# Ternary weights through GpSimd: the first of two operations moved, four G buffers, twelve places for up, the third weight summed in the first stage, attention rows loaded two tiles ahead

## The reference

```python
qkv = grouped_linear(x, w_qkv, None)           # 8 groups of 128 -> 384
out = softmax(q * D**-0.5 @ k.T) @ v           # 16 heads, D = 64, 2048 tokens
x = layernorm(x + grouped_linear(out, w_proj, b_proj))

def weight_quant(w):
    scale = 1.0 / clip(mean(abs(w)), 1e-5)     # one mean over all 4096 x 1024
    return clip(round(w * scale), -1, 1) / scale
def bitlinear(x, w): return act_quant(x) @ weight_quant(w).T
h = silu(bitlinear(x, w_gate)) * bitlinear(x, w_up)
y = layernorm(x + bitlinear(h, w_down))
```

## Time and profile before

| | us |
|---|---|
| three runs: median (lowest to highest) | 1289.52 (1288.72 to 1291.1) |
| the profiled execution, all cores | 1290.59 |
| its span on the slowest core (core 4) | 1289.0 |
| spans of the other cores | 1278.8 to 1287.9 |
| PE busy on core 4 | 1149.7 |
| DVE / ACT / POOL busy | 911.7 / 616.9 / 117.4 |

### The profile page before, as it was taken

How to read it: one execution, slowest core, us unless ns; L and a number is a source line. 1 busy time by engine, 2 the same in 40 slices (tenths; PEclk the granted TensorE clock), 3 DMA queues, 4 the chain that set the end, 5 groups by cost and what they waited for, 6 DMA issues and landing times.

```text
span 1289.0 us, 17877 instructions; the slowest of 8 cores (1278.8 to 1289.0 us)
## 1 busy us (share of the span) xinstructions
PE 1149.7 (89%) x6465; PEld 455.1 (35%) x6502; DVE 911.7 (71%) x1797; ACT 616.9 (48%) x679; POOL 117.4 (9%) x146
## 2 busy tenths in 40 slices
PE   3888998884898886599999999999999999999997
PEld 0333333321333222233333333333444444444443
DVE  4878889977899874474664547353789777977774
ACT  3798998884454487555555555554011111110110
POOL 1222112220001000010010001000000000000000
PEclk8999999997899898799999999999999999999999
DMA  8999934569799757242323223020523333233313
GB/s 237 307 326 316 325 102 158 176 195 318 239 250 226 208 138 241 90 92 65 92 70 78 86 39 117 5 70 1 145 89 81 89 82 99 72 89 66 82 34 82
DMA packets 129031, 179.74 MB, mean 139 GB/s; under 512 B 90033, under 2 KB 90801, under 8 KB 128946
## 3 DMA queue, kind: packets, MB, share of 16 engines
q1 hardware_dynamic: 120050, 149.52, 41.1%
q0 software_dynamic: 8896, 29.08, 7.4%
HBM read 127.41 MB, written 30.93 MB: 123 GB/s over the span
## 4 chain that ended last, share of the span: by engine, by line
PE 66%; DVE 13%; DMA 12%; ACT 5%; issue 4%; SPq 0%; POOL 0%; DVEq 0%; ACTq 0%; POOLq 0%
PE ps L802 32%; PE ps L897 16%; DMA stage<-wu 6%; PE ps L553 6%; PE ps L571 6%; PE ps L578 5%; ACT P L559 4%; DMA stage<-wd 3%; DVE asum L417 2%; DVE G L434 1%; ACT G L430 1%; DMA stage<-wg 1%; DMA stage<-xT 1%; DVE wgq L440 1%; DVE h L814 1%
## 5 line engine op out<-in xcount | busy, mean ns | idle before, releaser
L559 ACT ACTIVATE P<-ps 128x1024 bf16<-128x1024 f32 x512 | 492.5, 1021 | 236.6 <-PE ps L553 234.9
L808 ACT ACTIVATE T<-ps,tsc 128x512 f32<-128x512 f32 x128 | 88.0, 687 | 376.3 <-PE ps L802 330.5
L802 PE MATMUL ps<-wgq,xqT 128*128 128x512 fp8e4 x1024 | 249.2, 383 | 15.2 <-DVE hm L840 5.2
L802 PE MATMUL ps<-wuq,xqT 128*128 128x512 fp8e4 x1024 | 250.0, 384 | 8.7 <-DVE h L814 8.6
L897 PE MATMUL ps<-wdq,hqT 128*128 128x512 fp8e4 x1024 | 229.9, 380 | 1.3 <-DVE wdq L440 1.3
L571 PE MATMUL ps<-P,onesb 128*64 128x512 bf16 x1024 | 206.3, 399 | 14.2 <-DVE DT L594 14.2
L553 PE MATMUL ps<-Q,K 64*128 64x512 bf16 x1024 | 175.0, 389 | 44.1 <-ACT P L559 34.7
L578 PE MATMUL ps<-P,V 128*64 128x512 bf16 x1024 | 199.9, 386 | 0.9 <-DVE RC L598 0.5
L802 PEld LDWEIGHTS ps<-wuq,xqT 128*128 128x128 bf16 x1024 | 97.0, 99 | 142.0 <-issue 35.3
L802 PEld LDWEIGHTS ps<-wgq,xqT 128*128 128x128 bf16 x1024 | 95.8, 98 | 144.9 <-issue 39.9
L897 PEld LDWEIGHTS ps<-wdq,hqT 128*128 128x128 bf16 x1024 | 97.4, 98 | 129.8 <-issue 17.8
(11 more groups left out here) (95 smaller groups left out, 703.1 us busy)
## 6 DMA issues: line engine op xcount, KB each, us to landing
stage<-wu SPq DMA_DIRECT2D x64, 512.0 KB, 12.2
stage<-wd SPq DMA_DIRECT2D x58, 512.0 KB, 5.5
stage<-wg SPq DMA_DIRECT2D x42, 512.0 KB, 19.1
stage<-xT SPq DMA_DIRECT2D x16, 512.0 KB, 13.6
XB<-x SPq DMA_DIRECT2D x16, 512.0 KB, 5.3
xp_s<-XB SPq DMA_DIRECT2D x16, 512.0 KB, 2.6
Y<-xp_s SPq DMA_DIRECT2D x16, 512.0 KB, 4.3
y<-Y SPq DMA_DIRECT2D x16, 512.0 KB, 2.6
```

The costliest lines, as they stand in the source:

```text
L559: exp_tok[i] = act.do(lambda e: e.activation(P_sb[i % 4][:, :], bank(sb, 2), AF.Exp, bias=-C0, scale=0.125), pv_tok.get(i - 4), t)
L802: tp = pe.do(lambda e, ic=ic, w=w, bk=bk: e.matmul(bank(bk), xqT[b][:, ic, :], W_sb[w][:, 8 * q + ic, sl], start=(ic == 0), stop=(ic == 7) ...
L808: ta = act.do(lambda e: e.activation(T[:, :], bank(gb), AF.Tanh, bias=0.0, scale=tsc[:, t:t + 1]), tp, T_free[k], sc_tok[t])
```

## The change

1. Both first ternary operations (L434 on DVE, L430 on ACT) become one operation on POOL, for all three weights: 96 instructions.
2. The limit stays on DVE, but is emitted two pieces behind its first operation (`second`, `limit`), and there are four G buffers. Paid for with one RB buffer in place of two.
3. up's terns use 12 places (0 to 7 and 18 to 21) where they used 8.
4. The credit in the first stage is 0.62 for every step. A tern now costs 0.75 in all, where it cost 1.55.
5. Only places 22 and up are held back, so down's sums go through places 0 to 7 in the first stage.
6. The first stage ends after 252 steps; places 22 to 29 are released at step 230.
7. Two `AT` buffers; a tile's rows are loaded two tiles ahead.

```diff
-    AT = alloc("AT", [128, 8, 128], BF16)[0]
+    AT = [alloc(f"AT{i}", [128, 7, 128], BF16)[0] for i in range(2)]
-    G1 = [alloc(f"G1{i}", [128, 1024], I8)[0] for i in range(2)]
+    G1 = [alloc(f"G1{i}", [128, 1024], I8)[0] for i in range(4)]
-    RB = [alloc(f"RB{i}", [128, 512], F32)[0] for i in range(2)]
+    RB = alloc("RB", [128, 512], F32)[0]
...
-    order += [("tern", 1, k, k % 8, True) for k in range(16)]
+    ring = list(range(8)) + [18, 19, 20, 21]
+    order += [("tern", 1, k, ring[k % 12], True) for k in range(16)]
...
-    order += [("sum", 2, k, ring[n % 10], True) for n, k in enumerate(rest)]
+    order += [("sum", 2, k, n % 8, True) for n, k in enumerate(rest)]
...
-            if hold[0] and w == 2:
+            if hold[0] and s_ >= 22:
                 return
...
-            b = g1_n[0] % 2
+            b = g1_n[0] % 4
             g1_n[0] += 1
-            if w == 2:
-                t = act.do(lambda e, w=w, src=src, b=b: e.activation(
...
-            else:
-                t = dve.do(lambda e, w=w, src=src, b=b: e.tensor_scalar(
...
+            t = pool.do(lambda e, w=w, src=src, b=b: e.tensor_scalar(
+                G1[b][:, :], src[:, :], wst[:, 8 * w + 2:8 * w + 3], 1.0, ALU.mult, ALU.min),
+                g1_tok[b], t_stat[w], load_tok.get(o))
             used(o, t)
+            second.append((w, k, b, t))
+            if len(second) > 2:
+                yield limit()
...
+    def limit():
+        w, k, b, t = second.popleft()
+        g1_tok[b] = dve.do(lambda e: e.tensor_scalar(
+            W_sb[w][:, k, :], G1[b][:, :], -1.0, 1.0, ALU.max, ALU.min, saturate=False),
+            t, t_qkv_last[0] if w == 2 else None)
+        t_tern[(w, k)] = g1_tok[b]
+        return 0.75, None
...
-            pace = 0.55 if 0 not in t_red else 0.75 if ast[0] < 230 else 0.95
+            pace = 0.62
...
-    for i in range(0, 256, 2):
+    for i in range(0, 252, 2):
...
+        if i == 230:
+            hold[0] = False
+            for s_ in range(22, 30):
+                stage_tok[s_] = t_qkv_last[0]
+            load_more()
```

More of the change, by code:

```diff
@@ L305, in build @@
     order += [("tern", 0, k, k, False) for k in range(22)]
-    order += [("tern", 1, k, k % 8, True) for k in range(16)]
-    order += [("tern", 0, k, k % 8, True) for k in range(22, 24)]
+    ring = list(range(8)) + [18, 19, 20, 21]
+    order += [("tern", 1, k, ring[k % 12], True) for k in range(16)]
+    order += [("tern", 0, 22, 4, True), ("tern", 0, 23, 5, True)]
     order += [("tern", 1, k, k % 8, True) for k in range(16, 24)]
@@ L328, in build @@
     t_red = {}
-    g1_tok = [None, None]
+    g1_tok = [None] * 4
     g1_n = [0]
@@ L416, in weight_ops @@
             if kind == "sum":
+                while second:
+                    yield limit()
                 t = dve.do(lambda e, w=w, k=k, src=src: e.tensor_reduce(
@@ L425, in weight_ops @@
                 continue
[L426 removed]
+            b = g1_n[0] % 4
             g1_n[0] += 1
[L429 to L443 removed]
+            t = pool.do(lambda e, w=w, src=src, b=b: e.tensor_scalar(
+                G1[b][:, :], src[:, :], wst[:, 8 * w + 2:8 * w + 3], 1.0, ALU.mult, ALU.min),
+                g1_tok[b], t_stat[w], load_tok.get(o))
+            used(o, t)
+            second.append((w, k, b, t))
+            if len(second) > 2:
+                yield limit()
+        while second:
+            yield limit()
+    second = deque()
+    def limit():
[5 more added lines that the diff above has]
+        return 0.75, None
     later = []
@@ L964, in build @@
         bgstep(1.0)
[L965 to L969, removed]
     gu_on[0] = True
@@ L1005, in need_weights @@
                 run_later(force=True)
+                while totals:
+                    totals.pop()(7)
+            assert not wdone[0] or (w, k) in t_tern
     for kind, t in seq:
@@ L1017, in build @@
                 load_at(8)
+                load_at(9)
             proj_half(t, 0)
@@ L1023, in build @@
                 load_tile(t + 1)
-                if t + 1 != 8:
-                    load_at(t + 1)
+                if t + 2 < 16 and (t + 2) // 8 == t // 8:
+                    load_at(t + 2)
         elif kind == "GU":
@@ L1031, in build @@
                 if t == 0 and oc == 7:
+                    while 2 not in t_red:
+                        credit[0] = 1.0
+                        weight_step(credit)
                     hqT_alias[0] = [stage_tok[6], stage_tok[7]]
@@ L1037, in build @@
         elif kind == "X":
-            need_weights(2, 31)
+            if t == 0:
+                for k in range(32):
+                    need_weights(2, k)
             if t < 2:
```

20 lines of the change are left out of this document (11 added, 9 removed).

## The result

The changed kernel takes 1517.7 us (median; 1289.1 before): the ratio is 1.177, with a 95% interval of 1.175 to 1.180. The forecast was 1274 us in a range of 1243 to 1310. Rival (a), a first operation on POOL that is longer than the cast, came true, and beyond the 1409 us that its upper end gave.

A forecast was written before the change was run, and what follows sets the result against it. PE was taken as the bound, busy 1149.7 of 1289.0 us. The terms summed as 1290.6 + 5.6 (first stage) + 4 (four steps) - 25 (down's weights) = 1275, or 1274 us as median; range 1243 to 1310.

The forecast's parts named there:

- Rival (a): POOL's first ternary operation is longer than the cast: 1306 us at 1.4 us, 1409 at 2.53; chance 0.30.
- POOL's duration: First ternary operation of 1024 elements on POOL: taken as the cast's 1.041 us, upper end 2.53.
- 90 us of time per us of G: Each microsecond more of POOL's first operation costs 64 us in gate's and up's terns, about 26 in down's.
- break-even at 1.21 us: The 15 us of gain are gone if POOL's first operation takes 0.17 us more, 1.21 us.
- The first stage up to the terns: Attention before gate's and up's terns: 6 us lost, step 62 at 107 us, first tern (step 132) at 179.
- Turns: Steps 132 to 206: POOL's first operations and DVE's limits exclude each other, 1.45 us per tern, 105 us instead of 76.5.
- The end of the first stage: Last 46 steps take 48 us, second tile's rows lie ready; gate's first matmul at 333 us, before 327.4: +5.6 us.
- Down's weights, -25 us: After gate's first matmul: 46 us lost to down's sums, terns and clock shrink to 21, so 25 us won.
- four steps, +4: Four more attention steps remain for the stages after the first, as PE's work there: +4 us.
- (b): One-input operations on POOL and DVE take no turns; time 1240 us; chance 0.12.
- Faster at 0.60: Whole kernel: chance 0.60 of being faster by over 0.2%; within 0.2% 0.08, slower 0.32.

The follow-up runs named there:

- after_cast: The changed kernel with POOL's first ternary operation replaced by a plain copy, without scaling and upper limit: 1306.5 us, ratio 1.014.
- cast_hold: after_cast with the release of places 22 to 29 moved back from step 230 to behind the first stage: 1293.1 us, ratio 1.004.
- gback_hold: after_gback with the release of places 22 to 29 moved back from step 230 to behind the first stage: 1289.0 us, ratio 1.001.
- after_gback: The changed kernel with only the first ternary operation given back to DVE (gate, up) and ACT (down): 1301.5 us, ratio 1.010.
- at_ahead: The kernel before with two AT buffers and rows loaded two tiles ahead, nothing else: 1288.6 us, ratio 0.9997.
- after: The changed kernel with all parts of the change, against the kernel before: 1517.7 us, ratio 1.177.
- probe2: The kernel before with POOL casts or multiplications meeting DVE limits or PSUM copies after its last store; limits between one multiplication-with-minimum's start and end took 0.68 us.

## Why the prediction was wrong, step by step

**POOL's duration: the step that failed.** "The nearest is the cast of 128x1024 from float32, 1.041 us ... I take that", with 2.53 us as upper end. It is 3.69, and the 64 terns for which the sum had 105 us take 259. The copy was near in size and far in kind; and the upper end was no bound, since it took AO's price per element as the worst that POOL does.

**90 us of time per us of G: near.** From after_cast to the changed kernel 211 us for 3.69 - 1.05 = 2.64 us, 80 per us. By stages, from the start of gate's first matmul: 366.8 to 510.7 us before it, 54 per us (64 predicted), and 934.5 to 1004.4 behind it, 26 (26 predicted). The break-even at 1.21 us was wrong, though, because there was no gain to use up: at the cast's own 1.04 us the changed kernel takes 1306.5 us, 1.4% more than before. So the forecast would have failed with its duration granted, by the steps that follow.

**The first stage up to the terns: right.** Step 63 stands at 106.93 us (108 by the forecast), gate's red at 178.12 (175), the terns start at 182.7 (179).

**Turns: right for the steady pair, wrong in the sum.** 1.45 us per tern was forecast and 1.44 is the steady pair in cast_hold. But the 80 steps from DT of step 127 to that of step 207 take 174.20 to 297.85 = 123.7 us there, and my sum for them was 111: the seven long limits, 25.6 us where seven turns are 10.2, are the 12 us and more. And what I did not set side by side: 1.45 us of turns is what DVE spends on both operations by itself, 0.745 + 0.694 = 1.44. All that the cast could win here was DVE's copies and norms fitting beside POOL's turns. In gback_hold, with both operations on DVE, the same 80 steps take 117.6 us: my 111 would have won 6 to 7, and the measured 123.7 loses 6. after_cast is 5 us slower than after_gback.

**The end of the first stage: wrong.** The prediction says of the second tile's rows that "with two buffers they lie ready", and puts gate's first matmul a microsecond behind the half tiles. It looked at the wait for AT alone. Behind it stood the norm and the transposition of the same rows: 7.75 us of waiting in at_ahead, 9.5 in gback_hold. From step 207 to gate's first matmul cast_hold takes 55.7 us, 8 more than forecast. In the kernel as changed the burst of loads makes it 19, at a price of 13 us as the copy shows it. The sum has no term for item 6's release at step 230, without a reason given, and it put loads ahead of a transfer on which PE waits.

**Down's weights, -25 us, and four steps, +4: right at the cast's duration, for a reason that has nothing to do with the move.** In cast_hold 1293.5 - 353.6 = 939.9 us lie behind gate's first matmul, by the sum 961.6 - 21 = 940.6. gback_hold has 940.6 there too, with the first operation on ACT; so the order won these 21 us, and gave them back ahead of that matmul, which starts at 349.1 us for 327.4. Added up, 1274 + 12 + 8 = 1294 against cast_hold's 1293.1; with the burst 1307 against after_cast's 1306.5. From there to 1517.7 are the 211 us for 2.64 us of G, which are measured and not forecast: in after itself 1004.4 us lie behind gate's first matmul, 64 more than the sum had.

**The rivals.** (a) was the right mechanism, at a chance of 0.30, with its bound too low. (b), no turns, is refuted by the 1.44 us pairs.

**The chances.** Faster at 0.60 leaned on a duration that no row showed. A range for it from 1.04 to 2.53 us gave 1274 to 1409 us, and even that I cut at 1310.

## What to carry to other kernels

A copy says nothing of what arithmetic costs on the same engine: where the trace lacks the operation, the range has to go well past the nearest row of another kind. Before work moves to an engine that takes turns with the one relieved, compare the pair's turn with the time that the first engine needs for both operations; here they were equal, and ACT, for which DVE's operations kept their medians (0.742 and 0.682 us, 0.741 and 0.680 without), won 8 us with a third of the work, where it had room. Look behind a wait for the next one in the same chain, and at each transfer that a queue of released loads is put ahead of.

## What was not expected of the hardware

POOL takes 1.04 us to cast 1024 float32 elements to int8, 2.85 us to multiply them, 3.70 us to multiply and compare them, whatever the output type. By the ends of the limits in probe2, its 3.7 us operation keeps DVE's limits out for about 1.1 us at its start and for at most 0.9 at its end, not in between; copies out of PSUM, 0.68 us throughout there, were never kept out. A limit that asks 0.10 us after a cast has begun can be kept out over that cast and two more, to 3.45 us, while one that asked at 0.45 us got its turn after the first. A DMA transposition issued in after_gback at 344.9 us, behind fifteen loads of 512 KB issued from 318.1 to 338.0, needed 10.5 us for its issue and 15.7 to its landing; issued ahead of them, in gback_hold, it had landed in under 4.
